# Shifting token rows by matmul instead of by DMA, and a pixel layer norm on ScalarE, in a deformable-convolution and STU block

## The reference

```
n = layernorm over channels (x)                     # per pixel, eps 1e-6
offset = conv3x3(n, offset_w) + b                   # 18 channels
mask   = sigmoid(conv3x3(n, mask_w) + b)            # 9 channels
val    = mask * bilinear(n at pixel + tap + offset) # 9 taps, 4 corners each
y      = batchnorm(einsum(val, weight))
x      = x + y * sigmoid(y)
t = tokens(x); u = layernorm(t)                     # 1024 tokens of 64 channels, eps 1e-5
for i, frac in (1, 2, 4, 8):                        # four prefixes of the sequence
    plus, minus = causal convolutions of u with 16 spectral filters (plain, sign-alternated)
    s_i = plus x M_plus[i] + minus x M_minus[i] + u, u[t-1], u[t-2] x M_u[i]
out = t + sum_i weight_i * s_i                      # one hot with its softmax parts
```

## Time and profile before

| | us |
|---|---|
| median of 3 runs | 545.5 (543.98 to 546.7) |
| the profiled execution | 545.57 |
| its span, first to last instruction | 543.4 |

### The profile page before, as it was taken

The page is one execution under the profiler, slowest core; times in us unless marked ns, Lnnn a source line. Parts: engine busy times, 40 slices in busy tenths (PEclk is TensorE's granted clock), DMA queues, the critical chain, the costliest instruction groups (busy, mean ns, idle before and its releaser), DMA issues.

```text
span 543.4 us, 7147 instructions
## 1 busy us (share of the span) xinstructions
PE 439.2 (81%) x2660; PEld 217.9 (40%) x2660; DVE 316.9 (58%) x768; ACT 206.4 (38%) x413; POOL 296.8 (55%) x295
## 2 busy tenths in 40 slices
PE   4986481438775995999989996976699699989997
PEld 3442441315443442444434342643344354534333
DVE  5759977999864959292738429677374934040000
ACT  2124120125543562434333343654356244424232
POOL 1067777778777777777777773777776000000000
PEclk9999595558897999799989998889699889999999
DMA  6943699832334333333333332333433000000000
GB/s 154 185 109 106 155 326 349 259 111 83 102 102 112 102 98 109 103 104 103 104 109 98 104 100 53 104 93 108 114 103 97 6 10 1 2 5 11 0 1 10
DMA packets 47746, 54.41 MB, mean 100 GB/s; under 512 B 28656, under 2 KB 38134, under 8 KB 47713
## 3 DMA queue, kind: packets, MB, share of 16 engines
q0 software_dynamic: 13824, 37.77, 23.6%
q1 hardware_dynamic: 27865, 13.94, 10.2%
q10 hardware_dynamic: 6024, 2.26, 1.9%
HBM read 50.12 MB, written 3.30 MB: 98 GB/s over the span
## 4 chain that ended last, share of the span: by engine, by line
PE 58%; DVE 24%; DMA 10%; issue 3%; ACT 2%; SPq 1%; DVEq 0%
PE bank L902 32%; DMA u<-u 9%; PE bank L919 7%; PE bank L848 3%; PE bank L779 3%; DVE G L459 3%; PE bank L838 3%; DVE sil L472 2%; PE bank L760 2%; DVE G L460 2%; PE bank L939 2%; PE bank L876 1%; DMA filt<-in_L_ffn_phi_dram 1%; DVE V L463 1%; DVE st L299 1%
## 5 line engine op out<-in xcount | busy, mean ns | idle before, releaser
L279 POOL DMA_INDIRECT G<-corner_table,idx x288 | 294.2, 1022 | 122.0 <-issue 86.2
L902 PE MATMUL bank<-filt,u 128*128 128x512 f16 x960 | 243.2, 397 | 46.5 <-DMA u<-u 38.4
L680 ACT COPY u_conv<-bank 64x512 f32<-64x512 f32 x256 | 148.3, 579 | 202.7 <-PE bank L902 198.7
L902 PEld LDWEIGHTS bank<-filt,u 128*128 128x128 f16 x960 | 89.5, 100 | 167.8 <-issue 49.9
L919 PE MATMUL bank<-u_conv,mixw 128*64 128x256 f32 (+1 forms) x640 | 79.2, 356 | 5.9 <-issue 5.9
L459 DVE TENSOR_TENSOR G<-G,bank 128x2304 f32<-128x2304 f32 x32 | 81.5, 2547 | 1.3 <-DMA G<-corner_table,idx 1.2
L463 DVE TENSOR_TENSOR V<-G 128x576 f32<-128x576 f32 x32 | 24.4, 761 | 67.9 <-PE bank L839 67.2
L919 PEld LDWEIGHTS bank<-u_conv,mixw 128*64 128x64 f32 x640 | 35.8, 137 | 52.1 <-issue 50.6
L460 DVE TENSOR_TENSOR G<-G 128x1152 f32<-128x1152 f32 x32 | 43.5, 1358 | 1.1
L471 DVE TENSOR_SCALAR expo<-expo 128x128 f32<-128x128 f32 x16 | 4.4, 274 | 59.4 <-ACT expo L654 59.1
L838 PE MATMUL bank<-ident_swap,V 128*128 128x128 f32 x128 | 22.3, 309 | 14.6 <-DVE V L463 12.1
(11 more groups left out here) (153 smaller groups left out, 308.5 us busy)
## 6 DMA issues: line engine op xcount, KB each, us to landing
filt<-filter_rows SPq DMA_DIRECT2D x16, 514.0 KB, 12.2
G<-corner_table,idx POOLq DMA_INDIRECT x288
corner_table<-n_uT SPq DMA_DIRECT2D x12, 128.0 KB, 3.5
mixw<-in_x_dram SPq DMA_DIRECT2D x2, 512.0 KB, 6.3
filt<-in_L_ffn_M_phi_plus_dram SPq DMA_DIRECT2D x4, 256.0 KB, 7.5
out_dram<-o_sb ACTq DMA_DIRECT2D x8, 128.0 KB, 2.0
filt<-n_L_ffn_M_phi_minus_dram ACTq DMA_DIRECT2D x2, 256.0 KB, 5.6
corner_table<-n_uT ACTq DMA_DIRECT2D x4, 128.0 KB, 4.8
```

The lines of the kernel that those rows point to most:

```text
L279: pool.indirect_dma_start(G[:, k, tap, :], None, corners[bp], bass.IndirectOffsetOnAxis(ap=idx[:, q % 2, k, tap:tap + 1], axis=0)).then_in ...
L680: act.copy(u_conv[C * par:C * par + C, g % 2, :, b2, p, :], conv_ps[par][rows].rearrange("c (k a) -> c k a", k=GROUP)).then_inc(conv_copie ...
L902: last = pe.matmul(conv_ps[par][:].rearrange("c (k a) -> c k a", k=GROUP), u16[:, NJ * bp + j2, hl, b2, par:par + 2].rearrange("s w c -> s ...
```

## The change

Three parts.

1. Slot 2 of `u16` is no longer made by DMA. A shift matrix `ladder` (f16, 128x256) is built once by DVE from the identity. `step_odd_tokens` stands inside `convolve(0)`, ahead of its last block: PE waits for `u_ready`, multiplies slot 0 with the ladder (one matmul of 256 columns, and a second one with the block before if j > 0) into the second convolution bank; ACT copies the result to slot 2 (`copy_stepped`, the first thing ACT does in a pass). `convolve(1)` now waits for that copy ahead of its first matmul, since it writes the same bank. SP's 14 DMAs are gone.
2. The pixel layer norm of image pair 1 goes from DVE to ACT: 16 activations that copy and sum, 16 that square and sum, 16 that scale, with two short steps on DVE between them (`pixel_means`, `pixel_scales`). The summed copies and the squares stand ahead of the mixing matrices' copies on ACT, the scaling behind them.
3. The prologue is reordered. DVE: `filter_rows` after `masks(0)`, `weights(0)` and `pixel_means`; `inverse_roots` and `main_weights` ahead of `weigh(0, 0, 1)`; `weigh(0, 1, 0)` and `finish(0, 0)` ahead of `offsets(1, 0)` and `offsets(1, 1)`. PE: the turns and the convolution of block 0's first values are put ahead of, and between, the two `convolve_offsets` of pair 1. ACT: the copies of pair 1's offsets follow in the new order.

```diff
@@ SP @@
-            sp.wait_ge(shift_zeroed, BP)
-            for q in range(NQ):
-                sp.wait_ge(u_ready, 2 * q + 2)
-                sp.dma_start(u16[0:P - 1, q, :, :, 2], u16[1:P, q, :, :, 0]).then_inc(u_shifted, 16)
-                if q % NJ:
-                    sp.dma_start(u16[P - 1:P, q, :, :, 2], u16[0:1, q - 1, :, :, 0]).then_inc(u_shifted, 16)
@@ DVE @@
+            dve.memset(ladder[:, 0:P - 1], 0.0)
+            dve.memset(ladder[:, 2 * P - 1:2 * P], 0.0)
+            dve.tensor_copy(ladder[:, P - 1:2 * P - 1], ident).then_inc(ladder_ready, 1)
...
+            def pixel_means():
+                dve.wait_ge(x_copied, 4)
+                dve.tensor_scalar(stat[:, 1, :], stat[:, 0, :], -1.0 / C, None, ALU.mult).then_inc(pixels_meant, 1)
+            def pixel_scales():
+                dve.wait_ge(pixels_squared, 1)
+                link(dve.tensor_scalar(stat[:, 3, :], stat[:, 2, :], 1.0 / C, LN1_EPS, ALU.mult, ALU.add))
+                rsqrt(stat[:, 4, :], stat[:, 3, :], stat[:, 5, :])
+                dve.tensor_tensor(stat[:, 0, :], stat[:, 1, :], stat[:, 4, :], ALU.mult).then_inc(pixels_scaled, 1)
...
-            filter_rows()
             masks(0)
             weights(0)
+            pixel_means()
+            filter_rows()
             weigh(0, 0, 0)
-            normalise_pixels(1, (0, 1))
+            pixel_scales()
+            inverse_roots()
+            main_weights()
             weigh(0, 0, 1)
             positions(1)
             weights(1)
-            inverse_roots()
-            main_weights()
+            weigh(0, 1, 0)
+            finish(0, 0)
             offsets(1, 0)
             offsets(1, 1)
-            weigh(0, 1, 0)
-            finish(0, 0)
             weigh(0, 1, 1)
@@ ACT @@
+            groups = [(jq, p, b2) for jq in range(NJ) for p in range(2) for b2 in range(2)]
+            def copy_and_sum_pixels():
+                for g, (jq, p, b2) in enumerate(groups):
+                    if g % 8 == 0:
+                        act.wait_ge(x_turned, 2 + g // 8 + 1)
+                    last = act.activation(x_tok[:, NJ + jq, p, b2, :], bank[g // 8][:, C * (g % 8):C * (g % 8) + C], ACT.Identity,
+                                          accum_out=stat[:, 0, g:g + 1])
+                    if g % 8 == 7:
+                        last.then_inc(x_copied, 1)
+            def square_pixels():
+                act.wait_ge(pixels_meant, 1)
+                for g, (jq, p, b2) in enumerate(groups):
+                    last = act.activation(squared[:, C * g:C * g + C], x_tok[:, NJ + jq, p, b2, :], ACT.Square,
+                                          bias=stat[:, 1, g:g + 1], accum_out=stat[:, 2, g:g + 1])
+                last.then_inc(pixels_squared, 1)
+            def scale_pixels():
+                act.wait_ge(pixels_scaled, 1)
+                for g, (jq, p, b2) in enumerate(groups):
+                    last = act.activation(n_tok[:, 2 * NJ - 1 - jq, b2, 1 - p, :], x_tok[:, NJ + jq, p, b2, :], ACT.Identity,
+                                          bias=stat[:, 0, g:g + 1], scale=stat[:, 4, g:g + 1])
+                last.then_inc(n_ready, 1)
...
-            copy_pixels(1)
+            copy_and_sum_pixels()
+            square_pixels()
...
+            scale_pixels()
             for b2 in range(2):
                 lay_out_normalised(1, b2)
-            for b2 in range(2):
-                lay_out_offsets(1, b2)
...
             copy_values(0)
+            lay_out_offsets(1, 0)
             copy_convolved(0)
+            lay_out_offsets(1, 1)
...
+            def copy_stepped(n):
+                act.wait_ge(u_stepped, n + 1)
+                act.copy(u16[:, n, :, :, 2], conv_ps[1][:, 0:4 * C].rearrange("s (h b c) -> s h b c", h=2, b=2)).then_inc(u_shifted, 1)
             for n in range(NQ):
+                copy_stepped(n)
@@ PE @@
-            for b2 in range(2):
-                convolve_offsets(1, b2)
-            for b2 in range(2):
-                turn_offsets(1, b2)
...
-            for r in range(2):
-                turn_values(r)
-                convolve_values(r)
-                turn_convolved(r)
+            turn_values(0)
+            convolve_offsets(1, 0)
+            convolve_values(0)
+            convolve_offsets(1, 1)
+            turn_convolved(0)
+            for b2 in range(2):
+                turn_offsets(1, b2)
...
+            turn_values(1)
+            convolve_values(1)
+            turn_convolved(1)
...
+                def step_odd_tokens():
+                    pe.wait_ge(u_ready, 2 * n + 2)
+                    pe.wait_ge(conv_copied[1], START + STEPS * n)
+                    dst = conv_ps[1][:, 0:4 * C].rearrange("s (h b c) -> s h b c", h=2, b=2)
+                    last = pe.matmul(dst, ladder[:, P:2 * P], u16[:, n, :, :, 0], start=True, stop=(j == 0))
+                    if j:
+                        last = pe.matmul(dst, ladder[:, 0:P], u16[:, n - 1, :, :, 0], start=False, stop=True)
+                    last.then_inc(u_stepped, 1)
...
                         if j2 == j and i == 0:
-                            pe.wait_ge(u_ready, 2 * n + 2)
-                        if j2 == j and i == 1:
-                            pe.wait_ge(u_shifted, 16 * (7 * bp + 2 * j + 1))
+                            step_odd_tokens()
+                        if j2 == 0 and i == 1:
+                            pe.wait_ge(u_shifted, n + 1)
```

More of the change, by code:

```diff
@@ L77, in metaformer_kernel @@
         off_bias = sb("off_bias", [P, NOFF])
+        ladder = sb("ladder", [P, 2 * P], F16)
         w_off = sb("w_off", [P, TAPS, NCH])
@@ L184, in metaformer_kernel @@
         conv_copied = [sem(f"conv_copied{i}") for i in range(2)]
-        shift_zeroed, u_shifted, mix_scaled = sem("shift_zeroed"), sem("u_shifted"), sem("mix_scaled")
+        pixels_meant, pixels_squared, pixels_scaled = sem("pixels_meant"), sem("pixels_squared"), sem("pixels_scaled")
+        ladder_ready, u_stepped, u_shifted, mix_scaled = sem("ladder_ready"), sem("u_stepped"), sem("u_shifted"), sem("mix_scaled")
         group_mixed, mixed_copied, pass_turned = sem("group_mixed"), sem("mixed_copied"), sem("pass_turned")
@@ L307, in _ @@
             dve.memset(f_rows, 0.0)
-            for q in range(0, NQ, NJ):
-                dve.memset(u16[3 * P // 4:P, q, :, :, 2], 0.0).then_inc(shift_zeroed, 1)
+            dve.memset(ladder[:, 0:P - 1], 0.0)
+            dve.memset(ladder[:, 2 * P - 1:2 * P], 0.0)
             def reverse_pixels(bp):
@@ L315, in _ @@
             reverse_pixels(0)
+            dve.wait_ge(s_ident, 16)
+            dve.tensor_copy(ladder[:, P - 1:2 * P - 1], ident).then_inc(ladder_ready, 1)
             dve.wait_ge(s_woff, 32)
@@ L827, in _ @@
             last.then_inc(w_turned, 1)
-            pe.wait_ge(diag_ready, 1)
-            pe.wait_ge(off_copied, 2 * BP)
-            pe.matmul(scale_ps[:, 0:K], ones[:], f_diag[:], start=True, stop=True).then_inc(f_scale_ready, 1)
             def turn_values(r):
@@ L862, in _ @@
             pe.wait_ge(ones_ready, 2)
-            for r in range(2):
-                turn_values(r)
-                convolve_values(r)
-                turn_convolved(r)
+            pe.wait_ge(ladder_ready, 1)
+            turn_values(0)
[5 more added lines that the diff above has]
+                turn_offsets(1, b2)
+            pe.wait_ge(diag_ready, 1)
+            pe.wait_ge(off_copied, 2 * BP)
+            pe.matmul(scale_ps[:, 0:K], ones[:], f_diag[:], start=True, stop=True).then_inc(f_scale_ready, 1)
+            turn_values(1)
+            convolve_values(1)
+            turn_convolved(1)
             pe.wait_ge(f_scale_done, 1)
```

## The result

The changed kernel takes 508.24 us in the median (507.72 to 509.03, 4 runs) against 545.71 (4 runs, one more than above); the ratio of the runs is 0.932, with an interval of 0.929 to 0.935. The profiled execution has a span of 506.3 us where before had 543.4: 37.1 us less. The forecast was 515.2 with a range of 508 to 523: right in direction, and inside the range by 0.24 us only. 30.4 us were forecast of the 37 that came.

A forecast was written before the change was run, and what follows sets the result against it. The prediction took PE's idle time at the DMA waits, 32.0 us in passes 1 to 7, plus slow-clock restarts, with gathers holding pass 1. Gains of 1.0 + 7.1 + 3.7 + 4.9 + 8.1 + 4.8 + 0.8 = 30.4 gave 515.2 us, range 508 to 523.

The forecast's parts named there:

- The cold restart: PE's first matmuls after a DMA wait run at a slow clock: 1.4 us more than the wait's length, each time.
- rival 1: Gathers don't hold pass 1, which then gives 8.3 us, and the prologue's 1 us shows: 508.9 us; chance 0.08.
- The step: The shift's extra matmuls on PE and exposed handovers with ACT cost 0.4 us per pass, bounds 0.2 and 1.2.
- Pass 1 held by the gathers: At i = 10 PE waits for block 2's last gather and DVE's work: 1.0 us gained of 8.3.
- Pass 4 by DVE's wait: DVE decides pass 4 and loses only its wait for PE to empty V: 4.9 us gained.
- POOL's long wait goes, later margins hold: POOL's 7.79 us wait at 335.67 vanishes; gathers leave passes 2 and 5 free by 2 and 1 us.
- The signs of being wrong: Wrong if pass 1 shrinks over 3 us, the prologue grows over 7, or POOL's pace changes.
- Parts 2 and 3 in the prologue: ACT's norm makes n_ready 4.1 us later; pass 0 starts about 1 us later, covered, cost counted 0.
- 2 (prologue too long): ACT's norm outgrows its cover by 3 to 6 us, or ACT's tables switch: 518 to 522 us; chance 0.12.
- 3 (a dearer step, cold clock kept): The shift costs 1.2 us per pass and half the cold restarts stay: 521 to 524 us; chance 0.12.
- 4 (the chip grants less to a denser PE): Denser PE is granted less clock and its matmuls stretch; at 0.90, 564 us; chance 0.03.
- 5 (hidden by other chains in passes 2, 5, 6): DVE's or the gathers' chain holds passes 2, 5 and 6 too: 517 to 521 us; chance 0.1.

The follow-up runs named there:

- part 1 taken out: Changed kernel with the odd tokens moved by DMA again, the rest kept: 546.3 us, ratio to before 1.002.
- the runs without eight gathers: Changed kernel and kernel before, each without the ninth tap's fetch in blocks 1 and 2: 501.4 us and 545.9 us.
- part 1 alone: Kernel before with only the shift on PE and ACT's copy in place of the DMAs: 512.8 us, ratio 0.940.
- filled waits: Kernel before with idle matmuls, result overwritten, in PE's waits for the DMA in passes 1 to 6: 533.8 us, ratio 0.982.
- part 2 undone: Changed kernel with the pixel norm of pair 1 back on DVE, the new order kept: 515.3 us, ratio 0.946.
- 18 additions: Changed kernel with 18 additions of 128x256 in DVE's idle time: 511.5 us with both inputs in SBUF, 509.1 with one in PSUM.

## Why the prediction was right or wrong

- **What bounds it.** Right: the chain's 49 us were not to be had, PE's idle time was the base. With it back (part 1 taken out) the time is that of before.
- **The cold restart, 1.4 us each.** This is the term that was mis-sized. I took it from one pair of passes, 3 and 7, and used it for all. It is 2.6 us in pass 2 (7.86 against 5.27), and passes 2, 5 and 6 gave 1.6, 1.6 and 1.6 us more than forecast; pass 3, whose own rows it came from, 0.2. With 2.6 for 1.4 in those three the forecast would have been 3.6 us lower. The measured time lies in the range only because the range reaches down to rival 1, which is refuted; that part is luck. The rows for it were in the trace of before: pass 2's turn at i = 3 comes 7.86 us after its wait, with 21 convolution matmuls between, while pass 3's comes 7.95 us after, with 27.
- **The step, 0.4 us.** Measured 0.2: two matmuls 0.11 apart and no gap. Over seven passes 1.4 us, in the direction of the miss.
- **Pass 1 held by the gathers.** Right in the main, and the runs without eight gathers show it on both sides. Of 8.3 us only 2.8 came. I had 1.0 with a bound of 2.3, as part 1's, with the gathers where they were. That gain isn't seen: the end of pass 1 follows block 2's last issue by 35.6 us before the change and by 35.4 after, and the last issue itself comes 2.0 us earlier, which I had excluded ("this no edit here shortens", "POOL's pace"). With part 1 alone and the last issue at 174.9, pass 1 gives nothing (49.9 us against 49.1). So the 1.0 was right for a reason that I hadn't given. This was the one false statement on mechanism: DVE's two-input operations lengthen a gather, so an edit on DVE does move POOL. The extra time of long gathers in block 0 is 2.4 us before and 0.8 after. Of the two gathers of 1.84 us there, one lay beside the norm that part 2 took off DVE, the other beside the first weighing, which now meets the gathers at another moment.
- **Pass 4 by DVE's wait.** Right: 5.0 for 4.9, and PE still waits 2.2 us for DVE at i = 10. Pass 3: 3.9 for 3.7. Pass 7: 1.2 for 0.8.
- **POOL's long wait goes, later margins hold.** Right: POOL isn't held after its start, and its last issue is at 410.7 (410 forecast). Passes 2 and 5 ran at PE's pace.
- **The signs of being wrong.** Pass 1 shrank by 2.8 us, just under the 3 that I had named. POOL's pace did change, by 2.0 us over 107 gathers, pass 2 starts 2.3 us earlier where I had allowed 2, and PE's idle time at i = 10 is 4.3 us and not 6: by these the account of pass 1 was in part wrong.
- **Parts 2 and 3 in the prologue.** The cost on ACT was put too high. The groups of ACT:

```profile
L619 ACT ACTIVATE n_uT<-x_tok,stat 128x64 f32<-128x64 f32 x16 | 5.4, 428 | 0.0
L612 ACT ACTIVATE filt<-x_tok,stat 128x64 f32<-128x64 f32 x16 | 5.3, 333 | 1.1 <-DVE stat L350 1.1
...
L604 ACT ACTIVATE x_tok<-bank 128x64 f32<-128x64 f32 x16 | 3.3, 270 | 0.0
```

  The summed copies took 3.3 us for 16 (6.4 forecast: copy and read overlap wholly, 0.20 us a pair), the squares 5.3 (6.4), the scaling 5.4 (5.3). PE starts to turn the normalised pixels at 63.75 (65.3 forecast) and the first SiLU is at 83.30 (84.8). Pass 0 starts 0.6 us earlier instead of 1 later. Square added no table load (one in each profile), so the Trainium skill's price for a switch of sets (ScalarE: Activation LUTs, Table sets: the hidden batching unit) didn't fall due. The estimate of 0.33 us each for the scaling, from the Trainium skill (same page, What ACT_TABLE_LOAD costs), is what was measured: 5.4 / 16 = 0.34.
- **Pass 0, +1.1.** Not from the change. The kernels whose pass 0 is that of before have 49.9 in one profile and 50.9 in others (the runs with filled waits and with fewer gathers), so both lengths occur with the same code of pass 0.
- **The rivals.** 1 (gathers don't hold) is refuted. 2 (prologue too long) is not what the changed kernel shows, but pass 0 does start 12 us later with part 3 and without part 2, mostly by the clock. 3 (a dearer step, cold clock kept) is refuted, the opposite came. 4 (the chip grants less to a denser PE): the clock was 1.00 in passes 2, 3, 5, 6 and 7. 5 (hidden by other chains in passes 2, 5, 6): refuted.

In sum, by pass: 30.4 forecast; 4.8 more from the clock in passes 2, 5 and 6 and the cheaper step, 1.8 from pass 1, 0.7 in passes 3, 4 and 7, less 0.5 net by the start and pass 0: 37.2 of 37.1 measured.

## What to carry to other kernels

Here a wait of TensorE cost its length and a restart at the slow clock, and the restart was 1.4 us in one place, 2.6 in another and 9.6 in the kernel with part 2 undone. So read it in each place where it occurs, from the matmuls behind the wait, and don't carry it over from one. When a wait on the main chain is removed, look for the stream that ran with no idle time of its own, even if nobody waited for it: here POOL's gathers, which took two thirds of one pass's gain, and which every edit ahead of them then reached the end through. And where an in-order engine hosts another chain's step and waits for it, try taking it later: moving one small turn from i = 10 to i = 13 was worth another 10 us here.

## What the hardware showed that I had not expected

- A gather's issue on POOL takes 0.95 us, and up to 2.10 (part 1 alone, at 81.67) beside a DVE operation with both inputs in SBUF, ending 0.82 us after that operation; beside one with an input in PSUM it stays at 0.95 (18 additions, the four scalings of the mixing matrices, the weighing's first pass). The time over 0.95 us is 21 us of POOL in the changed kernel.
- PE's restart after idle time of 7.26, 6.08, 2.66 and 7.12 us in passes 1, 2, 3 and 5 cost about 1.5, 2.6, 1.4 and 2.7 us up to the turn at i = 3 (each against the same matmuls at full clock). The cost doesn't follow the length of the wait, and I can't say from these rows what it follows. After a wait of 4.15 us in the prologue of the kernel with part 2 undone the clock stayed at 0.50 for 22 us of unbroken work, at a cost of 9.6 us.
- Sixteen pairs of a 64-column activation and the read of its sum, from PSUM, take 0.20 us a pair; with a bias read from a column and the source in SBUF 0.33.
